# GpSimd computes the next pair's low part of x before a pair's four row scatters, instead of between the second and the third

## What is computed

```python
q = relu(x @ Wq.T + bq); k = relu(x @ Wk.T + bk); v = x @ Wv.T + bv      # 16 heads of 16
q_ = concat([q * sin, q * cos]); k_ = concat([k * sin, k * cos])
kv = einsum('nld,nlm->ndm', k_, v)
z  = 1 / maximum(einsum('nld,nd->nl', q_, k_.sum(axis=1)), 1e-4)
x  = layernorm(x + (einsum('nld,ndm->nlm', q_, kv) * z) @ Wo.T + bo)
topv, topi = top_k(x @ router_w.T, 2); gate = softmax(topv)
x  = layernorm(x + sum_e gate[:, e] * (gelu(x @ w1[e].T) @ w2[e].T))
```

## Time and profile before

| | us |
|---|---|
| median of 3 runs | 869.43 (869.2 to 871.21) |
| the profiled execution, its own time | 865.97 |
| its span in the trace | 864.2 |
| PE busy | 800.2 (93%) |
| DVE busy | 576.6 (67%) |
| ACT busy | 460.9 (53%) |
| POOL busy | 424.9 (49%) |

### The profile page before, as it was taken

The page is one execution under the profiler, slowest core; times in us unless marked ns, Lnnn a source line. Parts: engine busy times, 40 slices in busy tenths (PEclk is TensorE's granted clock), DMA queues, the critical chain, the costliest instruction groups (busy, mean ns, idle before and its releaser), DMA issues.

```text
span 864.2 us, 22025 instructions
## 1 busy us (share of the span) xinstructions
PE 800.2 (93%) x6684; PEld 735.2 (85%) x6684; DVE 576.6 (67%) x1816; ACT 460.9 (53%) x1044; POOL 424.9 (49%) x545
## 2 busy tenths in 40 slices
PE   4998998999989976999999999999999999999990
PEld 4888988888889865999999999998999999999980
DVE  3335888888878885677666667665444467777773
ACT  4565766666667644444455444443444445656653
POOL 3885566566656654544454445453322224444442
PEclk9999999999999997999999999999999999999995
DMA  6453133233323324323333332232422255666644
GB/s 201 155 167 102 42 102 112 75 104 105 110 75 108 113 84 123 113 83 100 104 101 95 104 94 82 84 114 80 125 75 86 83 212 196 221 228 221 220 166 171
DMA packets 56468, 106.64 MB, mean 123 GB/s; under 512 B 9261, under 2 KB 37551, under 8 KB 54448
## 3 DMA queue, kind: packets, MB, share of 16 engines
q1 hardware_dynamic: 41296, 63.25, 24.7%
q0 software_dynamic: 12624, 33.84, 10.7%
q10 hardware_dynamic: 2448, 8.26, 2.6%
HBM read 61.91 MB, written 44.32 MB: 123 GB/s over the span
## 4 chain that ended last, share of the span: by engine, by line
PE 77%; DVE 10%; ACT 4%; issue 4%; DMA 2%; SPq 1%; DVEq 0%; POOL 0%; ACTq 0%; POOLq 0%
PE PS L736 22%; PE PS L724 22%; PE PS L540 11%; PE PS L754 7%; PE PS L577 4%; PE PS L713 3%; DVE den L1054 2%; PE PS L629 2%; PE PS L613 2%; PE PS L600 2%; DVE o L1047 1%; ACT tcos L831 1%; DVE xtok L1150 1%; DMA xraw<-in_xT 1%; ACT vs L851 1%
## 5 line engine op out<-in xcount | busy, mean ns | idle before, releaser
L1669 POOL DMA_INDIRECT token_rows<-xg x135 | 134.8, 998 | 280.5 <-DVE xg L1403 255.2
L736 PEld LDWEIGHTS PS<-w,hT 128*128 128x128 f32 x1620 | 211.6, 189 | 12.0 <-issue 1.8
L724 PE MATMUL PS<-w,xgT 128*128 x810 | 221.8, 409 | 0.0
L736 PE MATMUL PS<-w,hT 128*128 x1620 | 217.3, 283 | 0.8 <-ACT hT L994 0.8
L724 PEld LDWEIGHTS PS<-w,xgT 128*128 128x128 f32 x810 | 143.0, 190 | 24.2
L994 ACT ACTIVATE hT<-PS 128x512 fp32r<-128x512 f32 x135 | 80.8, 598 | 135.3 <-PE PS L754 135.3
L1586 POOL DMA_INDIRECT expert_rows<-rows,idx x128 | 126.9, 991 | 44.6 <-issue 32.9
L990 ACT ACTIVATE hg<-PS 128x512 f32<-128x512 f32 x135 | 80.6, 597 | 121.2 <-PE PS L724 120.9
L1468 DVE TENSOR_TENSOR hT<-PS,hT 128x512 fp32r<-128x512 f32 x135 | 93.4, 692 | 75.2 <-ACT hT L994 75.2
L1395 DVE TENSOR_TENSOR xgT<-PS,xgT 128x256 fp32r<-128x256 f32 x135 | 57.0, 422 | 78.2 <-ACT xgT L960 77.0
L754 PE MATMUL PS<-cst,hg 128*128 128x128 f32 x540 | 81.0, 272 | 0.7 <-ACT hg L990 0.7
(11 more groups left out here) (179 smaller groups left out, 1302.1 us busy)
## 6 DMA issues: line engine op xcount, KB each, us to landing
xg<-expert_rows SPq DMA_DIRECT2D x135, 130.0 KB, 2.1
z<-token_rows SPq DMA_DIRECT2D x15, 1024.0 KB, 7.4
xraw<-in_xT SPq DMA_DIRECT2D x32, 256.0 KB, 3.3
xtok<-in_x SPq DMA_DIRECT2D x32, 256.0 KB, 3.1
out_y<-z ACTq DMA_DIRECT2D x15, 512.0 KB, 3.6
wraw<-in_w1T SPq DMA_DIRECT2D x7, 512.0 KB, 3.7
wraw<-in_w2T SPq DMA_DIRECT2D x7, 512.0 KB, 3.8
token_rows<-xg POOLq DMA_INDIRECT x135, 2.8
```

The costliest lines, as they stand in the source:

```text
L724: mm = nc.tensor.matmul(PS[:, gH, :], xgT[:, s % 2, a, k, :], w[:, bass.ds(e, 1), b, k * F:(k + 1) * F].rearrange("p o f -> p (o f)"), sta ...
L736: return nc.tensor.matmul(PS[:, gY, 0:D], hT[:, a, k, :], w[:, bass.ds(e, 1), b, HALF + k * D:HALF + (k + 1) * D] .rearrange("p o f -> p ( ...
L1669: nc.gpsimd.indirect_dma_start(yd, bass.IndirectOffsetOnAxis(ap=xg[:, XG_SLOTS[s % NXG], C_DST:C_GATE].bitcast(U32), axis=0), xg[:, XG_SLO ...
```

## The change

In GpSimd's `step` the call `x_low(i + 1, rep + 1)` moves from between the second and the third scatter to ahead of `scattered(j - 3)` and the first scatter. Its condition is the same, the amount of work too. No other engine's instructions change.

```diff
@@ GpSimd's step(u, rep)
                 scatters = rep > LAG + 2
+                if XLO_POOL <= rep + 1 < NPAIR:
+                    x_low(i + 1, rep + 1)
                 if scatters:
                     scattered(j - 3)
                     scatter(1 - slot, 0, 0)
                     scatter(1 - slot, 0, 1)
-                if XLO_POOL <= rep + 1 < NPAIR:
-                    x_low(i + 1, rep + 1)
-                if scatters:
                     scatter(1 - slot, 1, 0)
                     scatter(1 - slot, 1, 1)
                 if onward:
```

## The result

The changed kernel took a median of 875.05 us (871.98 to 876.65 in 11 runs), the kernel before beside it 869.2 us (867.77 to 871.21 in 11 runs). The ratio is 1.0065, with a 95% interval of 1.0054 to 1.0076: slower by 5.7 us where 12.5 us less was forecast. The profiled execution took 875.48 us.

A forecast was written before the change was run, and what follows sets the result against it. TensorE was taken to bound the kernel, held up in the first stage by VectorE's `den` waiting behind GpSimd's `x_low`. Gains 10.6 + 3.3 less 1.4 for clock made 12.5 us: 869.43 to 856.9 us, range 852.4 to 863.5.

The forecast's parts named there:

- Steps 1, 2 and 4: GpSimd `x_low` starts 2.7 us earlier after 0.4 us wait; `den` falls to 0.18 us; held `oh` costs 0 (bound 7.8 us).
- step 2: First stage: `den` falls from 1.18 to 0.18 us; TensorE can take 0.72 us of each 1.0, 10.6 us in all.
- Step 3: Rep 16 and 24: early `x_low` is over before `dls`, so TensorE's two L641 waits for `o` go, 3.3 us.
- Step 6: TensorE's clock: half-speed stretches after idle time may go or come later; 1.4 us off the gain, bounds +2 and -4.
- the fifth: GpSimd's four scatters in a row: last starts 0 to 0.4 us later, ScalarE's `normalise` covered; cost 0, bound 11 us.
- Slower: Rival: the last scatter lands too late for ScalarE's `normalise`, ahead of `tcos` of half 1; 877 us, chance 0.05.

The follow-up runs named there:

- e2: The changed kernel again, no edit, with a second trace, on the same chip as a rerun of the kernel before: 850.73 us.
- e15: The kernel before in its old order, with GpSimd's low part taken over 64 of 512 columns, chip 11: 848.25 us, ratio 0.9805.
- e1: The kernel before again, no edit, for a second trace: 864.79 us.
- e6: The changed kernel again, no edit, on chip 6: 849.8 us, ratio 0.9804 to the kernel before.
- e10: The changed kernel again, no edit, on chip 1: 849.95 us, ratio 0.9805 to the kernel before.
- e13: The changed kernel, no edit, loaded beside the kernel before alone, on chip 14: 850.14 us, ratio 0.9819.
- e5: The changed kernel, no edit, timed in five rounds on chip 3: 876.51 us against 869.21 for the kernel before, ratio 1.008.
- e17: The kernel before in its old order, with the low part over 64 of 512 columns, on chip 3: 866.63 us against 868.54, ratio 0.9976.
- e16: The changed kernel plus two tiny GpSimd power operations between the second and third scatter, on chip 13: 864.79 us against 869.67, ratio 0.9959.
- The gap version: The changed kernel plus two tiny GpSimd power operations between the second and third scatter: 851.38 to 853.22 us on four chips, 864.79 on chip 13.

## Why the prediction was wrong, step by step

The forecast of a gain came true on all four A chips that ran the changed kernel, and failed in the comparison of the result and on chip 3, because a cost was missing that only some of the chips here charge.

**What held.** Steps 1, 2 and 4 came as worked out. In e2 `x_low` starts within 0.2 us of the end of ScalarE's high part; its wait in the repetition below is 0.59 us where 0.4 was forecast. `den` fell to 0.18 us, `oh` rose to 0.70, and `o` of half 1 still has 0.18 us of idle time ahead of it (0.16 forecast), so the hold there costs nothing:

```profile
193.15 0.69 DVE L1115 TENSOR_TENSOR oh<-cst,ix 128x32 f32<-128x32 f32 x1
...
194.87 0.50 DVE L1047 SCALAR_TENSOR_TENSOR o<-PS,cst,tcos 128x272 f32<-128x272 f32 x1 [0.18 <-ACT tcos L831]
195.41 0.18 DVE L1054 TENSOR_SCALAR den<-o 128x32 f32<-128x32 f32 x1
```

The Trainium skill (SBUF — State Buffer, section "Who interferes with whom") has both: an operation of VectorE with two inputs in SBUF contends with one of GpSimd that reads SBUF, a `tensor_scalar` such as `den` can contend as well, and whichever comes first keeps the shared ports for its whole instruction. The `oh` at 0.70 instead of 0.19 us and the `den` of e15, short beside a short subtraction, agree.

**A term sized too small.** On A chips the gain was 14 to 16.5 us, not 12.5. The repetitions of the written-out middle fell from 10.3 to 10.5 us to 9.7, which is the 0.72 us each of step 2. But rep 13 and 14 fell from 10.9 to 9.7, 1.2 us each, and rep 31 from 8.32 to 7.10. Step 2 had taken one median-like repetition for all; the sum of the twenty distances gives 212.5 - 197.1 = 15.4 us between e1 and e2. Step 3 held in part: rep 16 fell from 12.15 to 9.73 us and rep 24 from 12.07 to 9.72, while the repetition behind rep 16 stayed at 11.33 and the one behind rep 24 rose from 11.33 to 12.86. Step 6 had allowed for something of the kind.

**The clock.** Step 6 had 1.4 us to lose. The stretches of 4 us from 104 to 312 us with a granted clock under 0.97 add up to 3.4 us of lost full speed in the first trace of the kernel before, 1.7 in e1, 3.8 in e2, and none in the slow trace of the changed kernel. The slow trace is thus not slow by the clock.

**The step that failed** is the fifth: "The scatters", "I take nothing; bound 0.6 x 19 = 11 us". It asked whether the scatters would take longer and whether their rows would land too late. Neither happened: they took 959 to 1214 ns, and ScalarE's `normalise` (L860) doesn't appear among the waits of that stretch in the slow trace. What it didn't ask is whether a denser run of scatters goes along with a cost to engines that have nothing to do with them. In the slow traces TensorE's increments come up to 3.7 and 3.8 us late beside it and TensorE itself pauses. Against the kernel before, the whole gain of 14 to 16 us that the A chips show is gone and 6 to 7 us more. By the twenty distances it is 218.5 us in the slow trace against 197.1 in e2, 21.4 us or 1.07 us each, of the 24.8 us between the two spans. The rival "Slower" gave 877 us at 0.05; its number came out, its mechanism did not.

**What is shown, and what is open.** Shown: the hold on `den` and its price (e15); that 850 or 876 us goes with the chip and not with the loading (e2, e6, e10, e13 against e5); that the early subtraction isn't needed for the late increments (e17), and that a pair of scatters is enough for them (e16). Indicated, but only by comparing one B chip with another: that breaking the run of scatters takes away about half of what the B chips charge, some 12 of 26 us left (e16 against e5). Open: why TensorE's increments are late there, what part the quicker pace of TensorE's work has in the loss, and whether the kernel before has late ones on a B chip as well, which its 4 us more and the pairs of e16 suggest and no trace shows. One candidate could not be tested. The same traces in which increments are late have lost a quarter of the records of increments, and every run here was recorded. The Trainium skill (NOTIFIC — the notification-queue block, section "7.1 Overflow: three behaviours, one of which stalls the engine") says that the block that writes such records holds up its producers rather than lose a record inside it, and that this may throttle an engine. If that is the cause, part of what the B chips charge is the price of being recorded; nothing here tells it from a lateness that would be there anyway. Where the records went missing says something, though. Before 100 us, ahead of the first scatters, all are there (1009 in the slow trace, 1013 in the first trace of the kernel before). From 100 to 330 us 1648 are left of 3134. From 350 to 800 us, in the second stage, the four traces with late increments hold 5015 to 5050 records instead of 6703, and after 335 us 38 to 50 of TensorE's increments are late or unrecorded; yet that stage, from its first matmul to the end, takes 538.6 to 540.5 us in them against 537.5 and 538.6 us in the traces of before and e2. So losing a quarter of the records doesn't by itself cost the time. The gap version is the only complete kernel here that is faster than the kernel before on both kinds, by 12 to 14 us on A chips (864.6 to 852.2, 864.9 to 851.4) and by 4.9 us on the one B chip; on A chips the changed kernel without the gap is faster still.

## What to carry to other kernels

A short operation of VectorE that always ends together with a GpSimd operation is probably paying for that operation's length; moving the GpSimd operation away, or shortening it, gave back 14 to 17 us on the A chips here. Before four GpSimd scatters are put in a row, time a version with some other GpSimd work between the second and the third: it cost 1.5 to 3.3 us where nothing was wrong, and the one chip of the other kind that ran it was 10 to 12 us below what the changed kernel took elsewhere. Time a change on more than one chip before its sign is believed. And look whether the profiled execution lies within the timed runs: here it lay below all of them, a sign from the start that trace and times came from unlike conditions.

## What the runs showed of the hardware

- Chips differ by kind: the kernel before 864.6 to 866.4 us on six, 868.5 to 869.7 on two; the changed kernel 849.8 to 850.7 on four and 876.5 on one. The sign of a change can depend on the chip.
- Beside GpSimd scatters TensorE's semaphore increments came late on two chips and in the trace of the result: from 75 to 335 us four traces have 63 to 83 that are late, by 0.8 to 2.1 us in the median and 3.8 us at most, and 1 to 15 without a record. In the traces of the A chips and the first trace of the kernel before none is over 0.3 us late and 0 to 3 have no record. Two scatters begun 1.4 us apart were enough (e16). TensorE also paused for up to 1.0 us ahead of instructions that have no wait.
- With them went records: 8960 to 9594 records of increments against 12202 to 12242.
- The hold between VectorE and GpSimd follows the length of the GpSimd operation: beside a 1.29 us subtraction `den` took 1.23 us, beside one of 0.33 us 0.185 us, bare 0.18 us.
